# A gated cross-attention block: stacks loaded in 8 KB runs, attention inputs in two alternating buffers

## Chip, core and metric

The kernel runs on one core of a Trainium2 chip. The metric is device time in microseconds (us), from the first to the last instruction of one execution; a run's number is the median over repeated executions. Five compute engines run their own instruction streams: TensorE (PE, matrix products), VectorE (DVE), ScalarE (ACT), GpSimd (POOL), and SyncE (SP), which here issues every DMA. They wait for each other through semaphores. Sixteen DMA engines carry the transfers.

## What is computed

Thirty-two sequences of 128 tokens, width 256, go through one decoder layer (self-attention A, cross-attention B on `ctx`, feed-forward C) added with a tanh gate, and then a gated FFN (E) with ternary weights and quantised activations:

```python
def _mha(q_in, k_in, v_in, ..., mask):          # 16 heads of depth 16
    q, k, v = (split heads of q_in @ wq + bq, k_in @ wk + bk, v_in @ wv + bv)
    scores = einsum('bhqd,bhkd->bhqk', q, k) / sqrt(16)      # masked
    return (softmax(scores) @ v) merged @ wo + bo
def layer(x, enc):
    x = ln(x + mha(x, x, x, ...))               # A
    x = ln(x + mha(x, enc, enc, ...))           # B
    return ln(x + relu(x @ ff_w1 + b1) @ ff_w2 + b2)         # C
x = x + tanh(g_xattn) * layer(layernorm(x), ctx)
x = x + tanh(g_ffn) * bitlinear_ffn(layernorm(x))            # E
```

## The kernel before

Two sequences form a group (T = 256 tokens); there are 16 groups, and the program is a software pipeline written out in full. `ORDER` lists, for each engine, the steps of one iteration with a lag: the step (2, ("B", "Q")) works in iteration t on group t - 2. Every engine walks its own list in order, so one late step holds all that stands behind it. The end of an iteration on one engine need not be that of another. Sixteen groups and lags up to 4 give 20 iterations.

Every float32 product is made of three float16 products of a high and a low part (`products`, L560). For the attention scores both parts are put into one contraction: the stack `stk[s, "Q"]` has, for each of the 16 heads, in partitions 0 to 63 four blocks of 16 depth channels (high, high, low, low), and `stk[s, "K"]` has (high, low, high, low). Partitions 64 to 127 hold mask and row-maximum rows. A score product then contracts 128 partitions at once.

The projections come out with 128 channels of (head, depth) in the partitions, so they are brought into the stack's form through DRAM:

1. `prep` makes `qk_AQ`, `qk_AK`, `qk_BK`, `qk_BQ` (128 partitions; part, chunk, token). For A/Q and B/K the low part comes from POOL (L1309), for the others from DVE (L1106).
2. `parts_out` (L443) writes 256 KB to `part_dram` with rows of one channel, 256 tokens, 512 bytes.
3. `parts_in` (L453) waits for that write and loads 4 transfers for each stack, 16 partitions x 16 heads x 512 bytes = 128 KB each: 512 KB for a stack.
4. `scores_max` (PE, L631 and L635) multiplies them for the row maxima; DVE takes the maximum of each (L1126), PE transposes it (L645), ACT and DVE split it in two float16 rows (`mT`, L903 and L1131), and SP writes the two rows into partitions 126 and 127 of the Q stack (L464). Then `scores` (L657, L662) can run, and ACT takes the exponentials (L896, L898).

PE reaches the first B maximum (2, ("B","smax",0,0)) with the wait for both B stacks; its first A maximum (0, ("A","smax",0,0)) waits for both A stacks; (2, ("B","S",1,0)) waits for the second pair of `mT_B` rows.

The inputs of A, B and C are `hin` (h0, h1, h2), one buffer each. A residual is needed long after the input's buffer is wanted again, so SP copies h0 and h1 to `hres_A` and `hres_B` (step "hres", L482, 256 KB each) and `W` (DVE L1153) adds from there. On SP the two copies stand ahead of B's four transfer steps, and the copy for B waits until `W` of the group before has read the last copy (DVE L1153).

Before the pipeline starts, SP loads biases and weights, ACT makes the high and DVE the low parts of the eight attention matrices (L781, L981); DVE then makes the bias rows (L994 to L997).

Of the kernel before, what the change touches and what calls it, by code (L numbers as in the profile page):

```python
# [6 lines left out]
F32 = mybir.dt.float32  # L7
# [202 lines left out]
def build(nc, x, ctx_in, mask_x, mask_s, g_x, g_f, w, out):  # L210
    with ExitStack() as stack:
# [10 lines left out]
        part_dram = {(s, t): nc.dram_tensor(f"parts_{s}{t}", (2, D, T), F16).ap() for s in "AB" for t in "QK"}  # L222
# [43 lines left out]
        hin = {"A": sb("h0", [P, G, D], F32), "B": sb("h1", [P, G, D], F32), "C": sb("h2", [P, G, D], F32)}  # L266
        hT = {s: [sb(f"hT_{s}{q}", [P, DC, T], F16) for q in (0, 1)] for s in "ABC"}
        hres = {s: sb(f"hres_{s}", [P, G, D], F32) for s in "AB"}
# [84 lines left out]
        hres_in = {s: sem(f"hres_in_{s}") for s in "AB"}  # L353
# [57 lines left out]
        def _(eng):  # L411
# [4 lines left out]
            for name, width in BIASES:  # L416
                eng.dma_start(bf[:, BCOL[name]:BCOL[name] + width], w[name].partition_broadcast(1)).then_inc(u_dma, 16)
# [19 lines left out]
            def parts_out(s, name, g):  # L437

                split = (masked_lo[s], g.at(1, 1)) if (s, name) in MASKED else read((s, name), g)
                taken = g.at(64)  # L440
# [77 lines left out]
        def _(eng):  # L518
# [53 lines left out]
            def prep(step, g):  # L572
# [4 lines left out]
                if name in ("T", "X", "TQ"):  # L577
# [6 lines left out]
                    else:  # L584
                        src = hin[s]
# [33 lines left out]
            def scores_max(step, g):  # L619
# [320 lines left out]
        def _(eng):  # L940
# [176 lines left out]
            def unit_step(step, g):  # L1117
# [29 lines left out]
                elif what == "W":  # L1147
# [10 lines left out]
            def beside(step, g):  # L1158
                kind, k = step[1], step[2]
                if kind == "F2":  # L1160
# [4 lines left out]
                    eng.scalar_tensor_tensor(res["C"][:, k, :], bank[:, 0:D], 1.0 / (WS * WS), hin["C"][:, k, :],  # L1165
# [57 lines left out]
        def _(eng):  # L1223
# [41 lines left out]
            def run(step, g):  # L1265
# [10 lines left out]
                elif kind == "N":  # L1276
# [4 lines left out]
                    if s == "A":  # L1281
                        wait(eng, *full(("B", "T"), g.back(1)))
# [72 lines left out]
```

## Time and profile before

| | us |
|---|---|
| runs | 1186.05, 1198.15, 1199.59 |
| median | 1198.15 |
| profiled execution | 1203.71 |
| its span (first to last instruction) | 1201.2 |

| engine | busy us | share of the span |
|---|---|---|
| PE | 920.2 | 77% |
| DVE | 793.9 | 66% |
| ACT | 629.5 | 52% |
| POOL | 606.3 | 50% |

The mean granted clock of PE is 0.89 of full speed; the 16 DMA engines are 43% busy with the kernel's own transfers, 84.43 MB in 138160 packets. No engine is busy all the time, so the sum of busy times doesn't give the end: what counts is which wait ends last at each place of the pipeline. Matmul records are lost here and there (a few per cent), so a busy time of PE is rather too small.

### The profile page before, as it was taken

The numbers are of one execution on the slowest core, as the hardware profiler recorded it, in microseconds if no ns is written. First come the engines' busy times: TensorE is split into PE (matmuls) and PEld (weight loads), VectorE is DVE, ScalarE is ACT, GpSimd is POOL, SyncE is SP. The second block draws the span as 40 slices with busy tenths as digits, with TensorE's granted clock in tenths as the row PEclk, the third lists the DMA queues.
The fourth block names the chain that finished last, engine by engine and source line by source line (L and its number), as shares of the span: only waits on it lengthen the run. The fifth ranks groups of instructions, "written<-read, shape, count | busy, mean of one in ns | idle before, by whom it ended". The sixth has DMA issues, their size and how long they took to land.

```text
span 1201.2 us, 26870 instructions
## 1 busy us (share of the span) xinstructions
PE 920.2 (77%) x10076; PEld 736.4 (61%) x10147; DVE 793.9 (66%) x1887; ACT 629.5 (52%) x996; POOL 606.3 (50%) x740
## 2 busy tenths in 40 slices
PE   1155568788888888788788888788898878796774
PEld 1134456666776767667577667667676767574552
DVE  8644365477778686757668676767686766675654
ACT  2222344465566565646456555656575646473543
POOL 6013255474647473726456464747373736563520
PEclk9966779889899999988989879999999988997886
DMA  5444454536272635345444517354554545404000
GB/s 152 111 100 62 72 81 68 84 62 74 70 81 77 79 74 80 53 74 89 72 63 92 71 54 86 50 96 66 81 81 81 81 72 76 78 28 62 20 10 9
DMA packets 138286, 86.14 MB, mean 72 GB/s; under 512 B 12552, under 2 KB 133551, under 8 KB 138160
## 3 DMA queue, kind: packets, MB, share of 16 engines
q1 hardware_dynamic: 138160, 84.43, 43.3%
q8 instruction: 82, 1.34, 0.6%
q14 instruction: 44, 0.36, 0.1%
HBM read 54.49 MB, written 20.98 MB: 63 GB/s over the span
## 4 chain that ended last, share of the span: by engine, by line
PE 28%; DMA 21%; DVE 15%; issue 9%; POOL 6%; ACT 5%; SPq 5%; POOLq 0%; DVEq 0%; ACTq 0%
DMA stk_BQ<-parts_BQ 10%; DMA stk_BQ<-mT_B 5%; PE lin_B L560 4%; SPq L453 4%; PE st L662 3%; PE lin_C L560 3%; PE smax L635 3%; DMA parts_BK<-qk_BK 2%; PE lin_A L560 2%; POOL elo L1272 2%; DVE nm_B L1126 2%; PE st L657 2%; DVE amc L1077 2%; DMA parts_BQ<-qk_BQ 2%; ACT ehi L898 1%
## 5 line engine op out<-in xcount | busy, mean ns | idle before, releaser
L1272 POOL TENSOR_TENSOR elo<-e,ehi 128x1024 f16<-128x1024 f32 x128 | 272.2, 2130 | 187.3 <-ACT ehi L898 187.0
L896 ACT ACTIVATE e<-st 128x1024 f32<-128x1024 f32 x128 | 130.1, 1016 | 106.9 <-PE st L662 106.7
L1126 DVE TENSOR_REDUCE nm_B<-smax 128x4 f32<-128x512 f32 x128 | 87.9, 686 | 90.0 <-PE smax L635 89.8
L1126 DVE TENSOR_REDUCE nm_A<-smax 128x4 f32<-128x512 f32 x128 | 87.8, 686 | 88.1 <-PE smax L635 80.1
L898 ACT ACTIVATE ehi<-st 128x1024 f16<-128x1024 f32 x128 | 130.3, 1018 | 0.0
L1309 POOL TENSOR_TENSOR qk_AQ<-qf_A,qk_AQ 128x512 f16<-128x512 f32 x16 | 18.5, 1156 | 220.1 <-ACT qk_AQ L850 220.1
L1258 POOL TENSOR_TENSOR lrs<-lve,neghalf 128x1 f32<-128x1 f32 (+1 forms) x112 | 69.0, 616 | 114.9 <-DVE lve L1052 114.9
L635 PE MATMUL smax<-stk_BK,stk_BQ 126*128 126x128 f16 x512 | 55.2, 236 | 59.5 <-DMA stk_BQ<-parts_BQ 56.2
L631 PE MATMUL smax<-mb,ident_big 128*128 128x512 f16 x128 | 56.4, 440 | 51.1 <-issue 39.9
L883 ACT ACTIVATE late<-lin_E,hcg 128x512 f32<-128x512 f32 x32 | 21.7, 677 | 122.5 <-PE lin_E L721 121.6
L635 PEld LDWEIGHTS smax<-stk_BK,stk_BQ 126*128 126x128 f16 x512 | 38.0, 105 | 68.8 <-DMA stk_BQ<-parts_BQ 57.9
L568 PE MATMUL lin_B<-ones,brows 128*128 128x256 f16 x96 | 29.5, 308 | 45.8 <-DVE hT_B L1093 41.9
L662 PEld LDWEIGHTS st<-stk_AQ,stk_AK 128*128 128x128 f16 x512 | 45.7, 110 | 22.8 <-issue 10.6
L635 PEld LDWEIGHTS smax<-stk_AK,stk_AQ 126*128 126x128 f16 x512 | 45.7, 110 | 21.8 <-issue 9.1
L657 PE MATMUL st<-mbT,ident_big 128*128 128x512 f16 x128 | 56.8, 444 | 2.9 <-DMA stk_AQ<-mT_A 2.9
L635 PE MATMUL smax<-stk_AK,stk_AQ 126*128 126x128 f16 x512 | 57.9, 244 | 0.0
L662 PE MATMUL st<-stk_AQ,stk_AK 128*128 128x128 f16 x512 | 56.8, 241 | 0.0
L662 PE MATMUL st<-stk_BQ,stk_BK 128*128 128x128 f16 x512 | 43.8, 235 | 9.9 <-DMA stk_BQ<-mT_B 7.6
L874 ACT ACTIVATE late<-late,magic_col,s 128x1024 f32<-128x1024 f32 x32 | 39.5, 1236 | 21.6 <-DVE s L1192 21.6
L631 PEld LDWEIGHTS smax<-mb,ident_big 128*128 128x128 f16 x128 | 13.5, 105 | 61.0 <-issue 47.3
L676 PE MATMUL av<-vhi_A,ehi 128*128 128x17 f16 x512 | 45.2, 171 | 3.1 <-POOL elo L1272 1.5
L676 PE MATMUL av<-vhi_B,ehi 128*128 128x17 f16 x512 | 43.7, 171 | 2.8 <-POOL elo L1272 2.5
(293 smaller groups left out, 3016.5 us busy)
## 6 DMA issues: line engine op xcount, KB each, us to landing
stk_AQ<-parts_AQ SPq DMA_DIRECT2D x64, 128.0 KB, 4.7
stk_AK<-parts_AK SPq DMA_DIRECT2D x64, 128.0 KB, 7.1
stk_BK<-parts_BK SPq DMA_DIRECT2D x64, 128.0 KB, 4.8
stk_BQ<-parts_BQ SPq DMA_DIRECT2D x64, 128.0 KB, 7.0
x_a<-in_x_dram SPq DMA_DIRECT2D x16, 256.0 KB, 2.9
cx<-in_ctx_dram SPq DMA_DIRECT2D x16, 256.0 KB, 7.3
parts_AQ<-qk_AQ SPq DMA_DIRECT2D x16, 256.0 KB, 2.3
parts_AK<-qk_AK SPq DMA_DIRECT2D x16, 256.0 KB, 2.9
```

The costliest lines, as they stand in the source:

```text
L453: eng.dma_start(stk[s, name][DH * j:DH * (j + 1), :, :], part_dram[s, name][q].rearrange("(h d) n -> d h n", d=DH)).then_inc(stk_in[s, nam ...
L560: mm = eng.matmul(dst, lhs(a, k), rhs(b, k), start=(start and at == 0), stop=(at == last))
L631: eng.matmul(smax[:, :], ident_big[:, :], mb[:, :].unsqueeze(1).to_broadcast([P, 4, P]), start=True, stop=True)
L635: mm = eng.matmul(smax[:, i * P:(i + 1) * P], stk[s, "Q"][0:XROW, h, tok], stk[s, "K"][0:XROW, h, tok], start=(s == "B"), stop=True, skip_ ...
L657: eng.matmul(st[:, k2 * 512:(k2 + 1) * 512], ident_big[:, :], mbT[:, :].unsqueeze(1).to_broadcast([P, 4, P]), start=True, stop=True)
L662: mm = eng.matmul(st[:, col:col + P], stk[s, "K"][:, h, tok], stk[s, "Q"][:, h, tok], start=(s == "B"), stop=True, skip_group_check=True)
L676: eng.matmul(dst, ehi[:, hf, i * P:(i + 1) * P], vhi[s][:, b, h, :], start=True, stop=False, skip_group_check=True)
L896: eng.activation(e32[:, hf, :], st[:, :], ACT.Exp, scale=SCORE).then_inc(e32_ready, 1)
L898: eng.activation(ehi[:, hf, :], st[:, :], ACT.Exp, scale=SCORE).then_inc(drain, 1)
L1126: eng.tensor_reduce(nm[s][:, 4 * part:4 * part + 4], smax[:, :].rearrange("p (h k) -> p h k", h=4), AX_X, ALU.max, negate=True).then_inc(d ...
L1258: eng.tensor_tensor(lrs[n][:, a:b], lve[n][:, a:b], neghalf[:, 0:b - a], ALU.pow).then_inc(ln_pow[n], 1)
L1272: eng.tensor_tensor(elo[:, hf, :], e32[:, hf, :], ehi[:, hf, :], ALU.subtract).then_inc(elo_ready, 1)
```

## The change

It has three parts.

- **Channel order.** The columns of the query and key matrices (and their biases) are permuted while they are split into high and low parts, so that partition p of chunk c holds depth p // 8 and head 2 * (p % 8) + c. With `part_dram` laid out as (part, partition, chunk, token), the 16 heads of one depth channel lie in one run of 8 KB.
- **Transfers.** A Q stack loads in 2 transfers of 32 partitions x 8 KB, a K stack in one of 32 and two of 16 partitions. The write goes in 1 KB rows. The bias vectors of q and k are permuted by the DMA that loads them.
- **Inputs.** h0 and h1 have two buffers each, used by even and odd groups. `W` adds from the input itself; the copies, their waits and `hres_A`, `hres_B` are gone.

```diff
-        (0, ("A", "M", 0)), (4, ("E", "DN", 1, 2)), (1, ("B", "hres")), (0, ("A", "hres")), (1, ("B", "K")),
+        (0, ("A", "M", 0)), (4, ("E", "DN", 1, 2)), (1, ("B", "K")),
...
-        part_dram = {... (2, D, T), F16 ...}
+        part_dram = {... (2, P, DC, T), F16 ...}
...
+        def input_of(s, g):
+            return hin[s][g.const % len(hin[s])]
+        def by_depth(mat, m):
+            return mat[:, :, m * P:(m + 1) * P].rearrange("p c (d e) -> p c d e", d=DH)
+        def of_raw(mat, m):
+            return mat.rearrange("p (c e m d) -> p m c d e", c=DC, m=DC, d=DH)[:, m, :, :, :]
+        BY_DEPTH = (0, 1, 4, 5)
+        LOADS = {"Q": 32, "K": 48}
...
+                if name[-1] in "qk":
+                    eng.dma_start(dst.rearrange("p (m d e) -> p m d e", m=DC, d=DH),
+                                  w[name].rearrange("(o e m d) -> o m d e", o=1, m=DC, d=DH),
+                                  allow_slow_non_contiguous=True).then_inc(u_dma, 16)
...
-                eng.dma_start(part_dram[s, name].rearrange("q (c p) n -> p (q c) n", p=P),
-                              qk_parts[s, name][:, :, :]).then_inc(part_out[s, name], 16)
+                eng.dma_start(part_dram[s, name].rearrange("q p c n -> p q (c n)"),
+                              qk_parts[s, name][:, :, :].rearrange("p (q c) n -> p q (c n)", q=2)).then_inc(
+                                  part_out[s, name], 16)
...
-                for j in range(4):
-                    q = j // 2 if name == "Q" else j % 2
-                    eng.dma_start(stk[s, name][DH * j:DH * (j + 1), :, :],
-                                  part_dram[s, name][q].rearrange("(h d) n -> d h n", d=DH)).then_inc(stk_in[s, name], 16)
+                rows = part_dram[s, name].rearrange("q (d e) c n -> (q d) (e c n)", d=DH)
+                for first, src in ((0, 0), (32, 0)) if name == "Q" else ((0, 0), (32, 16), (48, 0)):
+                    n = 16 if (name, src) == ("K", 16) or first == 48 else 32
+                    eng.dma_start(stk[s, name][first:first + n, :, :].rearrange("r h n -> r (h n)"),
+                                  rows[src:src + n, :]).then_inc(stk_in[s, name], 16)
...
-                elif kind == "hres":
-                    source = (ln_out[0], g.at(1, 1)) if s == "A" else (ln_bias[1], g.at(G, G))
-                    taken = read((s, "W", G - 1), g.back(1))
-                    eng.wait_ge(*source)
-                    wait(eng, *taken)
-                    eng.dma_start(hres[s][:, :, :], hin[s][:, :, :]).then_inc(hres_in[s], 16)
...
                 # high_part (ACT), n in BY_DEPTH; else as before
+                    for m in range(DC):
+                        a_ = eng.activation(by_depth(dst, m), of_raw(raw[n], m), ACT.Copy, scale=WS)
...
                 # low_part (DVE), n in BY_DEPTH; else as before
+                    for m in range(DC):
+                        for c in range(DC):
+                            i_ = eng.scalar_tensor_tensor(by_depth(lo, m)[:, c, :, :], of_raw(raw[n], m)[:, c, :, :], WS,
+                                                          by_depth(hi, m)[:, c, :, :], ALU.mult, ALU.subtract)
...
-                    wait(eng, *full(("A", "T"), g.back(1)))
-                    wait(eng, hres_in["A"], g.at(16))
+                    wait(eng, *full(("A", "T"), g.back(2)))
+                    wait(eng, *read(("A", "W", G - 1), g.back(2)))
...
-                    eng.wait_ge(hres_in[s], g.at(16, 16))
-                    eng.scalar_tensor_tensor(res[s][:, b, :], bank[:, 0:D], 1.0 / WS, hres[s][:, b, :], ALU.mult,
+                    eng.scalar_tensor_tensor(res[s][:, b, :], bank[:, 0:D], 1.0 / WS, input_of(s, g)[:, b, :], ALU.mult,
```

On SP, the transfers around the stacks of B read before as follows (one iteration; a row is line, instruction, target <- source, shape, and how often in a row):

```order
L482 DMA hres_B<-h 128x512
L482 DMA hres_A<-h 128x512
L443 DMA parts_BK<-qk_BK 128x4x256
L476 DMA stk_BK<-maskrow 1x16x256
L443 DMA parts_BQ<-qk_BQ 128x4x256
L453 DMA stk_BK<-parts_BK 16x16x256 x4
L453 DMA stk_BQ<-parts_BQ 16x16x256 x4
L464 DMA stk_AQ<-mT_A 1x16x128 x2
```

With the change the same place reads:

```order
L459 DMA parts_BK<-qk_BK 128x2x512
L494 DMA stk_BK<-maskrow 1x16x256
L459 DMA parts_BQ<-qk_BQ 128x2x512
L471 DMA stk_BK<-parts_BK 32x4096
L471 DMA stk_BK<-parts_BK 16x4096 x2
L471 DMA stk_BQ<-parts_BQ 32x4096 x2
L482 DMA stk_AQ<-mT_A 1x16x128 x2
```

The two copies are gone, so the write of `parts_BK` is the first of the group, and the eight loads are five.

Ahead of the pipeline DVE makes the low parts of the matrices; `w_AQ`, `w_AK`, `w_BQ`, `w_BK` are the ones that are permuted. Before:

```order
L981 SCALAR_TENSOR_TENSOR w_AQ<-late,w_AQ 128x512
L981 SCALAR_TENSOR_TENSOR w_AK<-late,w_AK 128x512
L981 SCALAR_TENSOR_TENSOR w_AV<-late,w_AV 128x512
L990 TENSOR_TENSOR late<-late,lin_E 1x256
L981 SCALAR_TENSOR_TENSOR w_AO<-late,w_AO 128x512
L981 SCALAR_TENSOR_TENSOR w_BQ<-late,w_BQ 128x512
L981 SCALAR_TENSOR_TENSOR w_BK<-late,w_BK 128x512
```

And with the change:

```order
L1001 SCALAR_TENSOR_TENSOR w_AQ<-late,w_AQ 128x128 x4
L1001 SCALAR_TENSOR_TENSOR w_AK<-late,w_AK 128x128 x4
L1005 SCALAR_TENSOR_TENSOR w_AV<-late,w_AV 128x512
L1015 TENSOR_TENSOR late<-late,lin_E 1x256
L1005 SCALAR_TENSOR_TENSOR w_AO<-late,w_AO 128x512
L1001 SCALAR_TENSOR_TENSOR w_BQ<-late,w_BQ 128x128 x4
L1001 SCALAR_TENSOR_TENSOR w_BK<-late,w_BK 128x128 x4
```

Four whole-matrix instructions have become sixteen quarters, at the same places of the list.

## Rows read from the trace of the kernel before

**Rows 1.** Waits of PE, whole span: waiter, releaser, total us, times, longest.

```profile
PE smax L635 <- DMA stk_BQ<-parts_BQ: 56.2, 16, 5.8
PE lin_B L568 <- DVE hT_B L1093: 41.9, 16, 3.4
PE smax L631 <- issue: 39.9, 15, 6.1
```

**Rows 2.** SyncE timeline, first and last of 15 writes of parts_BQ from 200 us.

```profile
200.63 0.37 SPq L443 DMA_DIRECT2D parts_BQ<-qk_BQ  x1
...
1092.44 0.36 SPq L443 DMA_DIRECT2D parts_BQ<-qk_BQ  x1
```

**Rows 3.** Busy us by stretch (PE, PEld, DVE, ACT, POOL), PEclk, DMA share, GB/s.

```profile
387.88:449.31 61.43, 52.61 (x628) 43.56 (x631) 46.45 (x115) 38.08 (x62) 36.47 (x46) 0.97 0.49 79
...
582.05:651.03 68.98, 56.06 (x631) 45.56 (x634) 46.71 (x115) 38.23 (x62) 36.73 (x46) 0.90 0.45 70
```

**Rows 4.** Waits of PE in the stretch 387.88:449.31 (clock 0.97).

```profile
PE smax L635 <- DMA stk_BQ<-parts_BQ: 2.8, 1, 2.8
PE smax L631 <- issue: 1.8, 1, 1.8
```

**Rows 5.** SyncE timeline around B's stacks, one iteration: start us, us, what.

```profile
647.92 0.52 SPq L482 DMA_DIRECT2D hres_B<-h  x1
...
649.17 1.19 SPq L443 DMA_DIRECT2D parts_BK<-qk_BK  x1
...
651.03 0.54 SPq L443 DMA_DIRECT2D parts_BQ<-qk_BQ  x1
653.00 1.80 SPq L453 DMA_DIRECT2D stk_BK<-parts_BK  x4
654.90 1.86 SPq L453 DMA_DIRECT2D stk_BQ<-parts_BQ  x4
```

**Rows 6.** POOL timeline of the same iteration: the low part of B's keys.

```profile
645.74 1.15 POOL L1309 TENSOR_TENSOR qk_BK<-qf_B,qk_BK 128x512 f16<-128x512 f32 x1
```

**Rows 7.** PE timeline of the same iteration: the first maximum of B.

```profile
664.51 0.61 PE L635 MATMUL smax<-stk_BK,stk_BQ 126*128 126x128 f16 x4 [4.36 <-DMA stk_BQ<-parts_BQ]
```

**Rows 8.** DMA rate in 40 slices of 656:664, loads of B's stacks.

```profile
GB/s 84 97 103 141 120 97 97 92 95 146 126 100 92 90 100 138 128 92 97 87 95 146 126 102 97 90 87 143 128 100 92 97 80 78 108 0 0 0 0 0
```

**Rows 9.** The same for 652.0:653.2, writes of parts, 512-byte packets.

```profile
GB/s 17 34 17 102 154 222 273 307 273 324 290 324 290 290 290 324 307 290 307 256 290 273 273 273 273 273 324 239 358 307 307 256 205 205 205 137 68 290 17 34
```

**Rows 10.** The same for 12:25, weight loads, 1 and 4 KB packets, 128 partitions.

```profile
GB/s 183 129 73 60 26 4 0 0 0 0 19 230 378 388 381 378 394 375 366 347 350 347 350 347 350 353 353 353 356 394 391 416 403 416 403 391 366 88 0 0
```

**Rows 11.** SyncE timeline around A's stacks, the same iteration.

```profile
609.53 0.94 SPq L443 DMA_DIRECT2D parts_AK<-qk_AK  x1
611.64 1.80 SPq L453 DMA_DIRECT2D stk_AQ<-parts_AQ  x4
613.54 1.87 SPq L453 DMA_DIRECT2D stk_AK<-parts_AK  x4
...
617.46 1.15 SPq L464 DMA_DIRECT2D stk_BQ<-mT_B  x2
```

**Rows 12.** PE timeline: the first maximum of A.

```profile
623.13 0.59 PE L631 MATMUL smax<-mb,ident_big 128*128 128x512 f16 x1 [3.08 <-issue]
```

**Rows 13.** DMA issues of the page: KB each, median us from issue to landing.

```profile
parts_BQ<-qk_BQ SPq DMA_DIRECT2D x16, 256.0 KB, 2.9
...
stk_BQ<-mT_B SPq DMA_DIRECT2D x64, 4.0 KB, 2.1
```

**Rows 14.** Stretch 6:7, `bvcol` loads: busy share in tenths by slice, packets.

```profile
DMA  0000011011221222122122222222221121121121
...
DMA packets 358, 0.00 MB, mean 1 GB/s; under 512 B 358, under 2 KB 358, under 8 KB 358
```

**Rows 15.** Timeline of the set-up: first ACT instruction, a low part on DVE.

```profile
17.09 1.28 ACT L781 ACT_TABLE_LOAD   x1 [17.09 <-DMA late<-in_L_xattn_s_wq_dram]
...
25.56 0.69 DVE L981 SCALAR_TENSOR_TENSOR w_AQ<-late,w_AQ 128x512 f16<-128x512 f32 x1
```

More of the change, by code:

```diff
@@ L221, in build @@
         out_v = out.rearrange("(g b) p d -> g b p d", b=G)
-        part_dram = {(s, t): nc.dram_tensor(f"parts_{s}{t}", (2, D, T), F16).ap() for s in "AB" for t in "QK"}
+        part_dram = {(s, t): nc.dram_tensor(f"parts_{s}{t}", (2, P, DC, T), F16).ap() for s in "AB" for t in "QK"}
         maskrow_dram = nc.dram_tensor("maskrow", (NG, T), F16).ap()
@@ L265, in build @@
         cx = sb("cx", [P, G, D], F32)
-        hin = {"A": sb("h0", [P, G, D], F32), "B": sb("h1", [P, G, D], F32), "C": sb("h2", [P, G, D], F32)}
+        hin = {"A": [sb(f"h0_{q}", [P, G, D], F32) for q in (0, 1)], "B": [sb(f"h1_{q}", [P, G, D], F32) for q in (0, 1)],
+               "C": [sb("h2", [P, G, D], F32)]}
         hT = {s: [sb(f"hT_{s}{q}", [P, DC, T], F16) for q in (0, 1)] for s in "ABC"}
-        hres = {s: sb(f"hres_{s}", [P, G, D], F32) for s in "AB"}
         qk_parts = {(s, t): sb(f"qk_{s}{t}", [P, 2 * DC, T], F16) for s in "AB" for t in "QK"}
@@ L439, in parts_out @@
                 split = (masked_lo[s], g.at(1, 1)) if (s, name) in MASKED else read((s, name), g)
-                taken = g.at(64)
+                taken = g.at(LOADS[name])
                 wait(eng, stk_in[s, name], taken)
                 eng.wait_ge(*split)
-                eng.dma_start(part_dram[s, name].rearrange("q (c p) n -> p (q c) n", p=P),
-                              qk_parts[s, name][:, :, :]).then_inc(part_out[s, name], 16)
+                eng.dma_start(part_dram[s, name].rearrange("q p c n -> p q (c n)"),
+                              qk_parts[s, name][:, :, :].rearrange("p (q c) n -> p q (c n)", q=2)).then_inc(
+                                  part_out[s, name], 16)
             def parts_in(s, name, g):
@@ L584, in prep @@
                     else:
-                        src = hin[s]
+                        src = input_of(s, g)
                         if s == "A":
@@ L780, in high_part @@
                 eng.wait_ge(u_raw[n], 16)
-                eng.activation(dst[:, :, :].rearrange("p c n -> p (c n)"), raw[n], ACT.Copy, scale=WS).then_inc(u_hi, 1)
+                if n in BY_DEPTH:
+                    for m in range(DC):
+                        a_ = eng.activation(by_depth(dst, m), of_raw(raw[n], m), ACT.Copy, scale=WS)
+                    a_.then_inc(u_hi, 1)
+                else:
+                    eng.activation(dst[:, :, :].rearrange("p c n -> p (c n)"), raw[n], ACT.Copy, scale=WS).then_inc(u_hi, 1)
             eng.wait_ge(u_const, N_CONST)
@@ L817, in prep @@
                     eng.wait_ge(ln_rstd[0], g.at(1, 1))
-                    wait(eng, *full(("A", "T"), g.back(1)))
-                    wait(eng, hres_in["A"], g.at(16))
-                    normalize(0, range(G), lambda k: x_a[:, k, :], lambda k: hin["A"][:, k, :])
+                    wait(eng, *full(("A", "T"), g.back(2)))
+                    wait(eng, *read(("A", "W", G - 1), g.back(2)))
+                    normalize(0, range(G), lambda k: x_a[:, k, :], lambda k: input_of("A", g)[:, k, :])
                     return
@@ L1281, in run @@
                     if s == "A":
-                        wait(eng, *full(("B", "T"), g.back(1)))
-                        wait(eng, hres_in["B"], g.at(16))
+                        wait(eng, *full(("B", "T"), g.back(2)))
+                        wait(eng, *read(("B", "W", b), g.back(2)))
                     else:
                         wait(eng, *read(("C", "F2", b), g.back(1)))
-                    eng.tensor_tensor(hin[nxt][:, b, :], tg[s][:, b, :], lnb[n][:, :], ALU.add).then_inc(ln_bias[n], 1)
+                    eng.tensor_tensor(input_of(nxt, g)[:, b, :], tg[s][:, b, :], lnb[n][:, :], ALU.add).then_inc(ln_bias[n], 1)
                 elif kind == "stat":
```

17 lines of the change are left out of this document (11 added, 6 removed).

## Prediction

> **What bounds the kernel now.** I read the shares of busy time first: PE 77%, DVE 66%, nobody full. So the length of an iteration is set by waits, and the view to go to is the waits of PE, the busiest engine. Over the whole span three of them are large [rows 1]: 56.2 us for the loads of B's query stack (16 times), 41.9 us for DVE's `hT_B`, and 39.9 us "issue" at L631. That last one isn't issue time: L631 is the first instruction of A's row maximum, behind the wait for both A stacks, and its DMAs run until it starts [rows 11, 12]. So some 96 us of PE's idle time are waits for stacks.
>
> Next the period. `parts_BQ` is written once per iteration; 15 of these writes, 14 periods, lie between 200.63 and 1092.44 [rows 2], 63.7 us each on average. They aren't equal: 61.43 us in a stretch whose granted clock is 0.97, 68.98 us in one with 0.90 [rows 3]. In the quick one PE still waits 2.8 us for the B stack and 1.8 us for the A stacks [rows 4]; in the slow one 4.36 and 3.08 us [rows 7, 12], and the clock falls to its lower level of 1.2 GHz for several us behind such pauses. I expect a period without the stack waits to look like the quick one less its two waits.
>
> **Why the stacks are late.** While B's stacks load, the DMA engines move about 110 GB/s [rows 8]. The writes of the parts, with the same 512-byte packets but 128 partitions, move about 290 [rows 9], and weight loads with 1 and 4 KB packets into 128 partitions 350 to 410 [rows 10]. So packets of 512 B alone don't explain 110. What is different in the stack loads is that a transfer ends in 16 partitions. I take it that the rate goes with the partitions reached: about 110 GB/s for 16, 220 for 32. The Trainium skill, "SBUF — State Buffer", section "Door 1: The DMA port swizzle", gives a cause: partitions 0 to 15 reach 4 of 16 ports (109 GB/s), 0 to 31 reach 8 (218 GB/s). The trace agrees for 16 partitions; for 32 no row here shows it. By that page the longer runs alone bring nothing, and K's two loads of 16 partitions stay slow; my sum has the same shape. The bounds by rows are 110 (nothing gained) and 410.
>
> **B's stacks, step by step** (the slow iteration). Before: `hres_B` goes out at 647.92, held until DVE's W has read the last copy; then `hres_A`, and `parts_BK` only at 649.17, though POOL has `qk_BK` ready at 645.74 + 1.15 = 646.9 [rows 5, 6]. K loads start to be issued at 653.00, the last Q load lands and PE goes on at 664.51, having stood since 660.15 [rows 7]. With the change:
> - `parts_BK` goes out at about 646.9, 2.3 us earlier, and is landed when `parts_BQ` is ready at 651.03, which doesn't move.
> - K's three issues (0.45 us each, 1.80 for four) follow at 651.5. Their data come behind the write of `parts_BQ`, from about 652.9: 256 KB at 220 and 2 x 128 KB at 110 GB/s, 1.2 us each, until 656.5.
> - `parts_BQ` is landed at 651.03 + 2.9 = 653.9 [rows 13]; Q's two issues end at 654.8. Its data, 2 x 256 KB at 220 GB/s, run to 658.9. Before, data ended at 663.0 (35 of 40 slices of rows 8) and PE went on 1.5 us later, so Q is usable at about 660.2.
> - PE wants it at 660.15. The wait of 4.36 us shrinks to between 0 and 0.5. At 410 GB/s there would be slack, and the time would be the same. At 110 GB/s 1 MB takes 9.5 us from 652.9 and 2 to 3 us of wait stay.
>
> **A's stacks.** `parts_AK` goes out at 609.53 [rows 11], unmoved (DVE sets it). Q's two loads follow, data from 611.5 to 613.9; K's issues wait for the landing of `parts_AK` at 612.4 and need 1.4 us, their data run from 613.6 to 617.2, usable at 618.7. PE wants them at 623.13 - 3.08 = 620.05: nothing left to wait, 1.3 us of slack. `cx` lies behind K in the queues, to 617.9. `mT_B`, issued 617.46 to 618.6, comes back in its normal 2.1 us [rows 13], 620.7 at the latest, when PE asks (620.5).
>
> **What doesn't bring time by itself.** The copies' 8 MB are 32 transfers of 0.7 us each beside other work; their worth is only the earlier `parts_BK`, and that is in B's sum. The second input buffers remove waits that were long over (two groups back instead of one); POOL and ACT don't show a wait there. `W` adds from another buffer of the same shape and costs the same. New waits: the input's writer waits for `W` of the group two back, which is an iteration old and more; it holds nothing. PE's list doesn't move.
>
> **What is left.** The quick period gives 61.43 - 2.8 - 1.8 = 56.8 us. DVE is busy 46.5 us of it, PE 52.6 [rows 3], and the 3.4 us wait for `hT_B` stays [rows 1]: 52.6 + 3.4 = 56.0, so 56.8 can be had, but nearly nothing under it. I add 0.5 for a rest of stack waits and short clock drops behind the `hT_B` pause: 57.3. Over 14 periods (63.7 - 57.3) x 14 = 90 us. Two more loads of B's stack lie outside them, at the start and at the end, 4.5 us each: 9.
>
> **Set-up.** Twelve more DVE instructions. A quarter matrix costs between 0.17 (a quarter of 0.69 us) and 0.69 us [rows 15]; nearer a quarter with its start, 0.3. Four matrices then cost 4 x (1.2 - 0.69) = 2 us, all on the path, as DVE's low parts run back to back into the bias rows. ACT's halves cost about as much, but ACT runs ahead of DVE there. The permuted bias loads are 4 x 256 elements of 4 bytes. The nearest row is `bvcol`, also 4-byte pieces: 358 packets in 1 us on 16 engines at a busy share near 0.15 [rows 14], so 7 ns of engine time and at most 45 ns of wall time each. Spread over all engines, 1024 pieces cost 0.5 to 3 us, hidden ahead of the weights, which ACT waits for until 17.09. If only one engine carried them, the weights behind them would come up to 46 us later. I take 2 us seen, so +4 in all; the range gets up to +20. The skill, "DMA: Bandwidth & Descriptors", section "Why a DMA increments its semaphore by 16 and not by 1", says that the engines used divide both patterns' slowest dimension, which here would be two engines, and its rules say a strided last dimension gives one descriptor per element. This speaks against the change: by it and the row's 7 to 45 ns, 512 pieces on an engine would take 4 to 23 us, and the set-up would come out at +5 to +20.
>
> **Sum**, against the profiled execution's own 1203.7 us: 1203.7 - 90 - 9 + 4 = 1109. The median of the runs is 0.46% below that execution, so about 1104.
>
> **Rivals.**
> - *The rate stays.* 8 KB rows into 16 or 32 partitions move no faster than 110 GB/s. For it: nothing in the trace shows a transfer into 32 partitions. Against it: 110 to 290 to 410 follow partitions. Then only the earlier `parts_BK` counts, some 1.5 us x 15 = 23, less 4: 1203.7 - 19 = 1185, as a median 1179, within 2%. Chance 0.12.
> - *The wait is taken over.* With PE early, DVE (46.5 us of 57) and POOL's `elo` decide who is late, or the pause at `hT_B` now meets a lower clock in most iterations (0.90 instead of 0.97 is 0.07 x 69 = 5 us of PE's speed in a period [rows 3]). Then the period is 60 to 61: 1203.7 - 38 to 52 - 9 + 4, a median of about 1150. For it: the 68.98 us periods themselves come of such drops. Against: the 61.43 us period has the 3.4 us pause and keeps 0.97. Chance 0.17.
> - *Slower.* A row of 8 KB written by one DMA engine into one partition is slower than sixteen rows of 512 B. It decides against the change where the stack loads land more than (24 + 99) / 15 = 8 us later than in my sum, which is below about 65 GB/s for the 1 MB of a pair. At 60 GB/s, 17.5 us for B's pair, PE would stand some 7 us at B and 5 at A instead of 4.4 and 3.1: about 1235. Nothing in the trace shows such a rate for large packets; chance 0.04.
>
> **Chances.** 0.67 for my forecast, whose own range is 1080 to 1130 (period 56 to 58.5, set-up +2 to +20), 0.17 for about 1150, 0.12 for about 1179, 0.04 slower. 2% of 1198 is 24 us, about what a measurement tells from no change, so faster means under 1174: 0.67 + 0.17 + a third of 0.12 = 0.88; within 2%: 0.08; slower 0.04. The range for 8 in 10 reaches from 1080 over the second case to 1160.
>
> **What would show it.** In the profile after: stack transfers at about 220 GB/s for 32 and 110 for 16 partitions; `parts_BK` issued when POOL's L1309 part ends; PE's wait for `stk_BQ` under 10 us in total instead of 56.2, "issue" at L631 under 10 instead of 39.9; the `hT_B` wait unchanged near 42; periods of 56 to 59 us; a mean clock above 0.93; first PE instruction of the pipeline (43 us before) within 2 to 20 us later. I am wrong if the stack rate is 110 all along, if the set-up grows by tens of us, or if the waits for stacks vanish and the period stays above 60.

## The result, and the profile after

| | before | with the change |
|---|---|---|
| median of the runs, us | 1195.13 (4 runs, 1186.05 to 1199.59) | 1072.97 (4 runs, 1067.78 to 1076.88) |
| profiled execution, us | 1203.71 | 1076.88 |
| its span, us | 1201.2 | 1075.0 |
| mean granted clock of PE | 0.89 | 0.92 |

The ratio is 0.898, with a 95% interval of 0.893 to 0.903. The change saves 122 us; I had forecast some 94, a time of 1104, and 1072.97 lies 7 us below the low end of my range, 1080.

First the page of the kernel after: busy time by engine, and the loads of B's query stack (count, KB each, median us from issue to landing).

```profile
PE 883.3 (82%) x10076; PEld 715.0 (67%) x10147; DVE 791.7 (74%) x1899; ACT 630.2 (59%) x1000; POOL 606.0 (56%) x740
...
stk_BQ<-parts_BQ SPq DMA_DIRECT2D x32, 256.0 KB, 5.8
```

DVE, ACT and POOL are busy as long as before (793.9, 629.5 and 606.3 us then). Only PE's own busy time fell, from 920.2 to 883.3 us, with the same list of products: its matmuls ran faster, which is the clock.

Next the waits of PE over the whole span (waiter, releaser, total us, times, longest), to be read beside [rows 1].

```profile
PE lin_B L580 <- DVE hT_B L1118: 40.6, 16, 3.4
...
PE st L669 <- DMA stk_AQ<-mT_A: 4.4, 7, 1.0
...
PE st L674 <- DMA stk_BQ<-mT_B: 4.2, 7, 1.4
...
PE smax L643 <- issue: 4.2, 2, 3.3
...
PE smax L647 <- DMA stk_BQ<-parts_BQ: 2.5, 1, 2.5
```

The wait for B's query stack went from 56.2 us in 16 waits to 2.5 us in one, the "issue" in front of A's maxima (L631 before, L643 now) from 39.9 to 4.2. The wait for `hT_B` stayed (41.9, now 40.6) and is the largest that is left.

The writes of `parts_BQ` mark the periods, as in [rows 2]. SyncE's timeline after (start us, us, what), first and last of the 15 from 190 us on:

```profile
194.11 0.37 SPq L459 DMA_DIRECT2D parts_BQ<-qk_BQ  x1
...
969.34 0.36 SPq L459 DMA_DIRECT2D parts_BQ<-qk_BQ  x1
```

Fourteen periods take 775.2 us, 55.4 each, where they took 891.8, 63.7 each. Of the 126.2 us by which the span is shorter, 116.6 are there, 6.5 ahead of the first write and 3.1 behind the last. The same stretch by windows (us, then busy us of PE, PEld, DVE, ACT and POOL with counts, PEclk, DMA share, GB/s), before:

```profile
200.63:1092.44 891.81, 748.15 (x8605) 612.87 (x8667) 625.55 (x1557) 520.08 (x835) 506.15 (x625) 0.93 0.47 74
```

and after, with one single period under it:

```profile
194.11:969.34 775.23, 711.98 (x8605) 591.97 (x8667) 621.38 (x1557) 518.77 (x835) 505.88 (x625) 0.97 0.33 75
...
585.40:639.69 54.29, 50.87 (x628) 42.54 (x631) 45.05 (x115) 38.05 (x62) 36.45 (x46) 1.00 0.35 80
```

PE's busy time for the same 8605 matmul records fell by 36.2 us, the clock rose from 0.93 to 0.97. In this stretch the two stack waits had been 46.9 us (B, 14 times) and 30.2 us (A, 13 times), and after neither is listed there. 77.1 and 36.2 make 113.3 of the 116.6 us. So, read from these two executions, about a third of the gain isn't the waits that went away but the higher clock of the work around them.

### The profile page after: what moved, and what is told of

Its sections match the earlier page's. It is cut to its first block, busy times and chain, and to the rows that moved or that the text cites. A ratio compares the mean times of both kernels' runs of the same rounds, so it can differ in the third digit from the quotient of the medians.

```text
span 1075.0 us, 26722 instructions
## 1 busy us (share of the span) xinstructions
PE 883.3 (82%) x10076; PEld 715.0 (67%) x10147; DVE 791.7 (74%) x1899; ACT 630.2 (59%) x1000; POOL 606.0 (56%) x740
## 4 chain that ended last, share of the span: by engine, by line
PE 44%; DVE 15%; issue 9%; POOL 7%; ACT 6%; DMA 6%; SPq 1%; POOLq 0%; DVEq 0%; ACTq 0%
PE lin_B L572 6%; PE lin_A L572 5%; PE lin_E L572 4%; PE st L674 4%; PE lin_C L572 4%; PE smax L647 3%; DMA stk_AQ<-mT_A 3%; POOL elo L1296 2%; PE st L669 2%; DVE amc L1102 2%; DMA stk_BQ<-mT_B 2%; ACT ehi L915 2%; DVE nm_B L1151 2%; ACT e L913 1%; PE lin_B L580 1%
## 5 line engine op out<-in xcount | busy, mean ns | idle before, releaser
L1333 POOL TENSOR_TENSOR qk_AQ<-qf_A,qk_AQ 128x512 f16<-128x512 f32 x16 | 18.5, 1155 | 156.2 <-ACT qk_AQ L867 156.2
L580 PE MATMUL lin_B<-ones,brows 128*128 128x256 f16 x96 | 29.2, 304 | 44.6 <-DVE hT_B L1118 40.6
L643 PE MATMUL smax<-mb,ident_big 128*128 128x512 f16 x128 | 53.5, 418 | 14.9 <-DVE nm_A L1151 10.2
L647 PEld LDWEIGHTS smax<-stk_AK,stk_AQ 126*128 126x128 f16 x512 | 43.1, 104 | 19.9 <-issue 5.6
L647 PE MATMUL smax<-stk_BK,stk_BQ 126*128 126x128 f16 x512 | 50.7, 222 | 6.6 <-DMA stk_BQ<-parts_BQ 2.5
L669 PE MATMUL st<-mbT,ident_big 128*128 128x512 f16 x128 | 50.9, 397 | 4.5 <-DMA stk_AQ<-mT_A 4.4
L647 PE MATMUL smax<-stk_AK,stk_AQ 126*128 126x128 f16 x512 | 54.1, 232 | 0.0
L674 PEld LDWEIGHTS st<-stk_AQ,stk_AK 128*128 128x128 f16 x512 | 41.0, 101 | 18.4 <-issue 2.5
L674 PE MATMUL st<-stk_AQ,stk_AK 128*128 128x128 f16 x512 | 51.2, 224 | 0.0
L580 PEld LDWEIGHTS lin_B<-ones,brows 128*128 128x128 f16 x96 | 10.1, 105 | 56.8 <-issue 43.0
L674 PE MATMUL st<-stk_BQ,stk_BK 128*128 128x128 f16 x512 | 40.1, 222 | 6.5 <-DMA stk_BQ<-mT_B 4.2
L692 PE MATMUL av<-vhi_A,elo 128*128 128x17 f16 x512 | 45.0, 171 | 0.0
```

The lines of the kernel that those rows point to most:

```text
L580: eng.matmul(dst, brows[:, col:col + P], ones16[:, 0:tokens], start=True, stop=False)
L643: eng.matmul(smax[:, :], ident_big[:, :], mb[:, :].unsqueeze(1).to_broadcast([P, 4, P]), start=True, stop=True)
L647: mm = eng.matmul(smax[:, i * P:(i + 1) * P], stk[s, "Q"][0:XROW, h, tok], stk[s, "K"][0:XROW, h, tok], start=(s == "B"), stop=True, skip_ ...
L669: eng.matmul(st[:, k2 * 512:(k2 + 1) * 512], ident_big[:, :], mbT[:, :].unsqueeze(1).to_broadcast([P, 4, P]), start=True, stop=True)
L674: mm = eng.matmul(st[:, col:col + P], stk[s, "K"][:, h, tok], stk[s, "Q"][:, h, tok], start=(s == "B"), stop=True, skip_group_check=True)
```

## The experiments

Each ratio is against the kernel before on the same chip, with its 95% interval. The theory that they test: the stack loads are paced by the partitions that a transfer reaches, PE's waits for them set the period, the copies bring little. The rivals: the copies or the shorter rows are what counts, or another wait takes over.

**e1: the kernel before without its copies.** Inputs in two buffers, `W` adds from the input, the stack transfers as before.

```diff
 # ORDER["SP"]
-(0, ("A", "M", 0)), (4, ("E", "DN", 1, 2)), (1, ("B", "hres")), (0, ("A", "hres")), (1, ("B", "K")),
+(0, ("A", "M", 0)), (4, ("E", "DN", 1, 2)), (1, ("B", "K")),
...
 # W, DVE
-eng.wait_ge(hres_in[s], g.at(16, 16))
...
-eng.scalar_tensor_tensor(res[s][:, b, :], bank[:, 0:D], 1.0 / WS, hres[s][:, b, :], ALU.mult,
+eng.scalar_tensor_tensor(res[s][:, b, :], bank[:, 0:D], 1.0 / WS, input_of(s, g)[:, b, :], ALU.mult,
```

> The kernel before with only the third part of the change: two input buffers, no copies; stacks still load as 4 transfers of 16 partitions x 16 x 512 B. Theory (the gain is the stacks' landing time, set by the partitions a transfer reaches): only the write of parts_BK moves ahead, PE's wait for stk_BQ falls from 56 us to about 30, the A wait stays near 40; 1160 to 1175 us. Rival (the 8 MB of copies in the DMA queues were what held things up): below 1130 us and stack landings clearly under 7 us.

Measured: 1187.6 us, ratio 0.989 (0.984 to 0.995), 13.5 us saved, which is under 2% but clear of no change. Waits of PE, whole span:

```profile
PE smax L631 <- DMA stk_BQ<-parts_BQ: 45.6, 16, 5.9
PE smax L627 <- issue: 41.5, 15, 6.0
```

The B wait lost 10.6 us of 56.2, the A wait nothing. An earlier `parts_BK` helps little while the 1 MB of the pair takes almost 9 us of data: the end of the loads hangs on the rate and on `parts_BQ`, which hasn't moved. I had expected two to three times as much. Taken alone, dropping the copies is worth about a ninth of the change's gain.

**e2: the change with the copies kept.** The reverse of e1, in the kernel after: one buffer for each input, copies and their waits back in their old places.

```diff
-(0, ("A", "M", 0)), (4, ("E", "DN", 1, 2)), (1, ("B", "K")),
+(0, ("A", "M", 0)), (4, ("E", "DN", 1, 2)), (1, ("B", "hres")), (0, ("A", "hres")), (1, ("B", "K")),
...
```

> The changed kernel with the copies put back: one input buffer each, both copies ahead of parts_BK on SyncE; loads in 8 KB runs. Theory: the stacks come 1.5 to 2 us later at B, which uses up the slack there, some 0.5 us of wait returns in an iteration; 1075 to 1095 us. Rival (the inputs carry the gain): above 1130 us.

Measured: 1077.2 us, ratio 0.899 (0.895 to 0.903), beside 0.898 (0.893 to 0.903) for the full change. The wait for B's query stack is 6.1 us in 5 waits instead of 2.5 in one. With the transfers in their new form there is slack in front of B, and what the copies take falls mostly into it. e1 and e2 together: the layout and the transfers carry the gain, the copies between nothing and some 13 us, depending on whether the loads are late anyway.

**e3: rows of 8 KB, but 16 partitions for each transfer.** Four transfers for a stack as before.

```diff
-LOADS = {"Q": 32, "K": 48}
+LOADS = {"Q": 64, "K": 64}
...
-for first, src in ((0, 0), (32, 0)) if name == "Q" else ((0, 0), (32, 16), (48, 0)):
-    n = 16 if (name, src) == ("K", 16) or first == 48 else 32
+for first, src in ((0, 0), (16, 0), (32, 16), (48, 16)) if name == "Q" else ((0, 0), (16, 16), (32, 0), (48, 16)):
+    n = 16
```

> The changed kernel with each stack in 4 transfers of 16 partitions x 8 KB. Theory (partitions reached set the rate): the rate stays near 110 to 140 GB/s, half the stack waits of before return, and lower clock behind them; 1110 to 1150 us. Rival (the length of the runs sets the rate): 1070 to 1080 us, as with 32 partitions.

Measured: 1120.84 us, ratio 0.936 (0.932 to 0.940). Waits of PE, and the DMA rate in 40 slices of 0.4 us from the issue of `parts_BQ`'s write (543.55:559.55):

```profile
PE smax L647 <- DMA stk_BQ<-parts_BQ: 19.9, 15, 4.0
PE smax L643 <- issue: 18.6, 15, 5.1
...
GB/s 21 0 256 338 389 287 41 287 41 143 184 0 287 41 123 205 0 246 82 123 205 0 12 49 0 0 0 0 0 0 0 0 0 0 0 0 0 0 0 0
```

The time is where the theory had it, but both waits are under half of what they were before, and the rate will turn out above the 110 to 140 GB/s expected: the longer rows help at 16 partitions as well. e4 turns the question round.

**e4: the partitions of the change, but rows of 512 bytes.** Even and odd heads are loaded apart, so every run in DRAM is one head's 256 tokens; ten transfers for a pair.

```diff
-LOADS = {"Q": 32, "K": 48}
+LOADS = {"Q": 64, "K": 96}
...
-    eng.dma_start(stk[s, name][first:first + n, :, :].rearrange("r h n -> r (h n)"),
-                  rows[src:src + n, :]).then_inc(stk_in[s, name], 16)
+    for c in range(DC):
+        eng.dma_start(stk[s, name][first:first + n, :, :].rearrange("r (e c) n -> r c e n", c=DC)[:, c, :, :],
+                      rows[src:src + n, :].rearrange("r (e c n) -> r c e n", c=DC, n=T)[:, c, :, :]).then_inc(
+                          stk_in[s, name], 16)
```

> The changed kernel with the same partitions in each transfer, but even and odd heads apart, so that every run is 512 B (twice as many transfers: 4 for Q, 6 for K). Theory: 32-partition transfers move about 200 GB/s also with 512 B runs, five more issues of 0.45 us cost about 1 us of landing; 1075 to 1100 us. Rival (run length): the rate falls back to 110 GB/s and the time to 1130 us or more.

Measured: 1098.71 us, ratio 0.915 (0.912 to 0.919). The two stack waits, the rate (535.77:551.77) and SyncE's issues of the same place:

```profile
PE smax L649 <- DMA stk_BQ<-parts_BQ: 15.2, 12, 4.1
...
PE smax L645 <- issue: 8.5, 7, 3.9
...
GB/s 0 0 266 340 78 224 172 214 137 96 87 170 69 113 101 228 128 245 196 159 220 42 13 41 0 1 0 0 0 0 0 0 0 0 0 0 0 0 0 0
...
536.23 3.82 SPq L472 DMA_DIRECT2D stk_BK<-parts_BK  x6
540.15 2.49 SPq L472 DMA_DIRECT2D stk_BQ<-parts_BQ  x4
```

For comparison the same 16 us of e1, whose transfers are those of before (510.31:526.31):

```profile
GB/s 0 0 201 284 213 257 172 138 142 101 92 137 100 96 134 102 95 138 99 92 141 99 92 152 91 84 53 9 4 0 0 0 0 41 0 0 0 0 0 0
```

and of the kernel after (529.65:545.65), with SyncE and PE in this iteration:

```profile
525.32 0.37 SPq L459 DMA_DIRECT2D parts_BK<-qk_BK  x1
...
530.11 1.34 SPq L471 DMA_DIRECT2D stk_BK<-parts_BK  x3
531.84 0.77 SPq L471 DMA_DIRECT2D stk_BQ<-parts_BQ  x2
...
539.50 0.38 PE L647 MATMUL smax<-stk_BK,stk_BQ 126*128 126x128 f16 x4
...
GB/s 0 0 266 325 392 164 410 143 184 143 123 205 61 205 164 225 225 48 14 0 0 0 41 0 0 0 0 0 0 0 0 0 0 0 0 0 0 0 0 0
```

In each row the first 262 KB are the write, and what follows is the pair's 1 MB (1.05 million bytes). Counted from where the write's bytes are used up to the last large slice, it takes about 8.7 us with 16 partitions and 512-byte rows (e1, 121 GB/s), 6.8 us with 16 partitions and 8 KB rows (e3, 154), 6.7 us with the partitions of the change and 512-byte rows (e4, 156), and 5.2 us with both (after, 200). Over thirteen iterations of each run the order is the same: 7.8 to 8.9, 6.2 to 7.0, 6.5 to 7.8 and 5.1 to 5.7 us.

A slice can hold parts of several transfers. What one transfer takes is read better from the landings of the query stack's loads: in the kernel after, the two are issued at 531.8 and 532.2 us and land 5.1 and 5.9 us later.

```profile
L471 SPq DMA_DIRECT2D stk_BQ<-parts_BQ x2: 302/362/422, 531.8 to 532.2; - x2
...
DMA to landing us min/median/max: 5.1/5.5/5.9
```

The same two lines for the query stack's four loads of e1, of e3 and of e4, each from the same iteration as above:

```profile
L455 SPq DMA_DIRECT2D stk_BQ<-parts_BQ x4: 392/444/447, 513.1 to 514.6; - x4
...
DMA to landing us min/median/max: 6.1/7.2/7.9
```

```profile
L471 SPq DMA_DIRECT2D stk_BQ<-parts_BQ x4: 368/420/421, 545.9 to 547.3; - x4
...
DMA to landing us min/median/max: 5.5/6.3/6.9
```

```profile
L472 SPq DMA_DIRECT2D stk_BQ<-parts_BQ x4: 542/607/608, 540.2 to 542.0; - x4
...
DMA to landing us min/median/max: 3.1/3.3/3.4
```

From one landing to the next it is 1.2 us for 256 KB in the kernel after, but 1.1 us for only 128 KB in e1 and 0.9 us for 128 KB in e3 (medians over all iterations: 1.1, 1.1 and 0.9). So a transfer into 32 partitions brings 1.7 to 2 times as much in the same time as one into 16, much as the theory says. But e3 shows that the rows count too: into the same 16 partitions 8 KB rows go in some 0.9 us where 512-byte rows take 1.1, and the pair moved a quarter faster (154 against 121). Whether that comes from fewer packets or from neighbouring transfers, into different partitions, overlapping more, these runs don't tell.

e4 can't give the rate of 512-byte rows into 32 partitions, only a lower bound. Its loads land a steady 3.1 to 3.4 us after their issue, the last as soon as the first, while in e1 they queue up and land 6.1 to 7.9 us after it. So in e4 SyncE sets the pace: ten issues take 6.3 us (five take 2.1 in the kernel after; I had counted 0.45 us for one), and one in 0.62 us is some 210 GB/s for Q's 128 KB transfers and 102 for K's 64 KB ones, which is what its slices hold there (196 in the 16th to the 21st, 106 in the 10th to the 15th). e4's 26 us over the kernel after are therefore at least in part the issues, not the row length.

With e1, e3, e4 and the kernel after, none of which has the copies, the two effects can be set side by side, as shares of the time before:

| saved | 16 partitions | 32 (K: 32 and 16) |
|---|---|---|
| 512-byte rows | 1.1% (e1) | 8.5% (e4, held back by its issues) |
| 8 KB rows | 6.4% (e3) | 10.2% (after) |

Either one alone gets most of the way, and they don't add up. e1 also keeps the write in 512-byte rows: that of `parts_BQ` lands after 2.8 us by the median there and after 2.2 in the kernel after, and the pair's data start some 0.3 us later behind it. That is small beside the 3.5 us by which the two differ in the data themselves. Not tried was a load into 32 partitions with the old channel order.

**e5: the kernel before with ten dummy products (128x512) on PE ahead of its wait for B's stacks.** Their output, in `smax`, is overwritten. This asks what a pause costs besides its own length.

```diff
+if s == "B" and (b, quad) == (0, 0):
+    wait(eng, drain, before)
+    for i in range(10):
+        eng.matmul(smax[:, :], ident_big[:, :], mb[:, :].unsqueeze(1).to_broadcast([P, 4, P]), start=True, stop=True)
 if quad == 0:
     for t in "QK":
```

> The kernel before, with ten extra products of 512 columns (2.2 us at full clock) on PE just ahead of the wait for B's stacks, written over afterwards: the wait stays as long as it was, but PE is busy for most of it. Theory (a stall costs its own length and then the lower clock behind it): the measured wait for stk_BQ shrinks by about 2 us each, nothing of this is time won, but drops of the clock behind it become rarer, mean clock 0.92 or more, and the kernel is 10 to 35 us faster than before although it does more. Rival (the lower clock costs nothing on the path, the gain of the change is only the stalls themselves): same time or up to 10 us slower.

Measured: 1186.71 us, ratio 0.989 (0.983 to 0.994). The wait for B's stack over the whole span and the steady stretch by windows:

```profile
PE smax L640 <- DMA stk_BQ<-parts_BQ: 17.4, 14, 3.1
...
199.58:1077.31 877.73, 770.71 (x8809) 617.44 (x8807) 622.35 (x1557) 519.60 (x835) 506.30 (x625) 0.95 0.48 75
```

PE does more work, gets nothing earlier, and the kernel is 13 us shorter (under 2%, but the interval leaves out no change): the clock of the stretch is 0.95 instead of 0.93, the period 62.7 instead of 63.7 us. The mean clock of the whole execution is 0.91, just short of the 0.92 that I had expected. Part of what a stack wait costs is therefore the slower work behind it.

**e6: the kernel after, three small DVE operations made one column at a time.** `amc`, `hcg` and `kap` (128x2) stand directly ahead of `hT_B` on DVE. In the period shown they take about three to seven times what they took where they were quickest (0.17, 0.21 and 0.22 us). The timelines of DVE and POOL in the kernel after, and `amc`'s durations in it (ns: shortest, median, longest):

```profile
633.12 1.24 DVE L1102 TENSOR_SCALAR amc<-am 128x2 f32<-128x2 f32 x1
...
634.47 0.56 DVE L1106 TENSOR_SCALAR hcg<-amc,kg 128x2 f32<-128x2 f32 x1
635.07 0.75 DVE L1108 SCALAR_TENSOR_TENSOR kap<-hcg,ku,amc 128x2 f32<-128x2 f32 x1
635.75 0.68 DVE L1118 TENSOR_TENSOR hT_B<-lin_E,hT_B 128x512 f16<-128x512 f32 x1
...
632.21 2.12 POOL L1296 TENSOR_TENSOR elo<-e,ehi 128x1024 f16<-128x1024 f32 x1
634.30 0.71 POOL L1303 TENSOR_TENSOR tg_B<-nrm_B,lng 128x256 f32<-128x256 f32 x1
635.09 0.72 POOL L1311 TENSOR_TENSOR h<-tg_B,lnb 128x256 f32<-128x256 f32 x1
...
L1102 DVE TENSOR_SCALAR amc<-am x16: 169/1255/1925, 238.9 to 1048.7; 128x2 f32<-128x2 f32 x16
```

`amc` ends (634.36) when POOL's `elo` ends (634.33), `hcg` (635.03) with the next POOL instruction (635.01), `kap` (635.82) with the one after (635.81). It isn't chance: over the kernel these are 48 instructions, and 44 of them end within 0.04 us of the end of a POOL instruction; the other four have none beside them and are the quickest.

The edit (`hcg` is split like `amc`, and `kap` is also written with two scalars for each partition instead of a second input):

```diff
-eng.tensor_scalar(amc[:, :], am1[:, :], 1e-5, 1.0 / QMAX, ALU.max, ALU.mult).then_inc(q_small, 1)
+for k in range(G):
+    i_ = eng.tensor_scalar(amc[:, k:k + 1], am1[:, k:k + 1], 1e-5, 1.0 / QMAX, ALU.max, ALU.mult)
+i_.then_inc(q_small, 1)
...
-eng.scalar_tensor_tensor(kap[:, :], hcg[:, :], ku[:, 0:1], amc[:, :], ALU.mult, ALU.mult).then_inc(q_small, 1)
+for k in range(G):
+    i_ = eng.tensor_scalar(kap[:, k:k + 1], hcg[:, k:k + 1], ku[:, 0:1], amc[:, k:k + 1], ALU.mult, ALU.mult)
+i_.then_inc(q_small, 1)
```

> The changed kernel, with the three small 128x2 VectorE instructions ahead of hT_B (amc, hcg, kap) each split in two of 128x1, the last with a per-partition scalar in place of its second tensor. Theory (what is left of PE's waits, 3.4 us for hT_B in an iteration, is on the path, and it is so long because these instructions end only when a GpSimd instruction beside them ends): amc, hcg, kap fall from up to 1.9, 0.7, 1.1 us to 0.2 to 0.4 us, the wait for hT_B from 41 to below 20 us in all; 1030 to 1055 us. Rival (another wait takes its place, or the GpSimd instructions have nothing to do with it): 1065 to 1080 us.

Measured: 1038.24 us (1037.04 to 1042.45), ratio 0.865 (0.861 to 0.868), the fastest kernel here. Durations of two of the operations in e6, the wait of PE, the steady stretch:

```profile
L1103 DVE TENSOR_SCALAR amc<-am x32: 142/149/155, 237.7 to 1008.5; 128x1 f32<-128x1 f32 x32
...
L1113 DVE TENSOR_SCALAR kap<-hcg,ku,amc x32: 264/268/274, 238.3 to 1009.3; 128x1 f32<-128x1 f32 x32
...
PE lin_B L580 <- DVE hT_B L1123: 11.8, 16, 1.7
...
191.00:932.04 741.04, 704.89 (x8669) 582.55 (x8667) 592.87 (x1599) 519.36 (x835) 505.17 (x625) 1.00 0.35 79
```

Twice as many instructions, each steady, and together 15.7 us instead of 45.0 over the kernel; the wait for `hT_B` falls by 28.8 us, and the time by about 35 (by the two ratios, each against its own runs of the kernel before, by 40). The rest fits PE's busy time in the steady stretch, 704.9 instead of 712.0 us at a clock of 1.00 instead of 0.97, and somewhat more than that for each record, as e6's stretch holds 64 more of them. The Trainium skill, "SBUF — State Buffer", section "Who interferes with whom", says that VectorE and GpSimd share one pair of ports, that a `tensor_scalar` in a two-port mode and a GpSimd instruction hold it against each other for a whole instruction, and that an operation with two SBUF inputs contends with a GpSimd instruction that reads SBUF. The rows agree: the 128x2 forms end with POOL's instruction, the 128x1 forms vary by no more than 13 ns, though a POOL instruction runs beside 45 of their 48 pairs.

**e7: the kernel after with twelve dummy products ahead of PE's wait for `hT_B`** in (B, Q), the counterpart of e5.

```diff
 src = hT[s]
+if step == ("B", "Q"):
+    for i in range(12):
+        eng.matmul(bank[:, :], ident_big[:, :], mb[:, :].unsqueeze(1).to_broadcast([P, 4, P]), start=True, stop=True)
 eng.wait_ge(*read((s, src_name), g))
```

> The changed kernel with twelve extra products of 512 columns (2.6 us) on PE ahead of the wait for hT_B, written over afterwards. Theory of the clock: in the changed kernel the drops that are left start behind this pause, so they get rarer, mean clock in the steady part above 0.98, and the time falls by 5 to 20 us. Rival (the pause doesn't set the clock, or the clock isn't on the path): same time within 5 us or slower.

Measured: 1067.85 us (1064.66 to 1068.93), ratio 0.888 (0.884 to 0.892).

```profile
PE lin_B L580 <- DVE hT_B L1122: 6.5, 10, 0.7
...
195.81:961.30 765.49, 738.68 (x8835) 597.53 (x8835) 623.70 (x1557) 520.66 (x835) 506.59 (x625) 1.00 0.34 76
```

The dummy products fill the wait, they don't shorten it, yet the clock is 1.00 and the period 54.7 instead of 55.4 us. So some 0.7 us of the kernel after's period is lower clock behind the `hT_B` pause. By the medians it is 5 us of the whole, against 35 in e6, by the ratios 12 against 40: most of what e6 took is the pause itself.

## Why the prediction was right, and where it wasn't

**Stack rate (right for 32 against 16 partitions, wrong on the rows).** In 512-byte rows 16 partitions move about 110 to 121 GB/s (e1), and 32 at least 196 (e4). In the kernel after, Q's transfers of 256 KB land 1.2 us apart, about 218, where I had 220. The pair's data took 5.2 us where I had 6.0 (652.9 to 658.9). The Trainium skill, "SBUF — State Buffer", section "Door 1: The DMA port swizzle", gives 109 and 218; these rows agree. Where I followed it to "the longer runs alone bring nothing", e3 says otherwise: 6.8 instead of 8.7 us, the two waits at 38.5 us instead of 96.1, and 80 us saved without a single 32-partition transfer (up to 13 of them are the copies). With 8 KB rows the wider transfers add some 45 us to that.

**B's and A's stacks (right).** `parts_BK` goes out at 525.32, when POOL's low part is ready (its L1333 ran until 525.25); the issues take 1.34 and 0.77 us; the last Q load, issued by 532.6, lands 5.8 us later by the median in the profile's DMA issues, at about 538.2; PE starts the first maximum at 539.50, 9.9 us behind the write of `parts_BQ`, without a wait. I had both at 9.1 us behind that write; it was 8.6 and 9.9. At A 4.2 us of "issue" are left over the whole kernel. So a transfer time 0.8 us too long hardly showed at B, where PE came later than the data in either case.

**Copies (right).** e2: within the measurement. "Their worth is only the earlier `parts_BK`" holds. For e1 I had still expected 1160 to 1175. The prediction's own 1.5 us a period (23 us) gives 1175, and even that is too much: measured was 0.7 us less wait per iteration and 13.5 us in all.

**Periods (the step that failed).** The term for a period without stack waits was too large, because it kept PE's busy time of a stretch in which part of the work ran at the lower clock. I wrote 61.43 - 2.8 - 1.8 = 56.8 "but nearly nothing under it", since 52.6 + 3.4 = 56.0, and added 0.5. Measured: 55.4 on average, 54.29 in the one shown above. The term was 1.9 us too large, 27 us over 14 periods:
- The 52.6 us that PE is busy weren't a floor. Windows of 1 us of the kernel before, right behind the 2.8 us wait of that quick stretch (PE goes on at 400.07):

```profile
400.00:401.00 1.00, 0.71 (x5) 0.59 (x7) 0.40 (x1) 0.00 (x0) 0.00 (x0) 0.62 0.00 0
401.00:402.00 1.00, 1.00 (x6) 0.52 (x5) 0.84 (x2) 0.00 (x0) 0.00 (x0) 0.50 0.00 0
402.00:403.00 1.00, 1.00 (x9) 0.72 (x7) 0.14 (x1) 0.00 (x0) 0.00 (x0) 0.50 0.00 0
403.00:404.00 1.00, 1.00 (x11) 0.90 (x9) 0.42 (x1) 0.00 (x0) 0.00 (x0) 0.67 0.00 0
404.00:405.00 1.00, 1.00 (x11) 0.89 (x10) 0.97 (x4) 0.00 (x0) 0.00 (x0) 1.00 0.00 0
```

  PE is busy there at 1.2 GHz for a little over 3 us, and about 1.7 us of speed are gone (52.61 against 50.87 us for 628 records at 1.00). I took the wait out of the stretch and left the slow work behind it in. In the kernel after, the other pause, at `hT_B`, still costs clock: read by the microsecond, the stretch has ten drops, all at or close behind that pause, 43 us at the lower clock together (one short drop in e6, and one in e7). So on average 0.65 us of the 1.7 come back: 711.98 / 8605 is 82.7 ns for a record, 52.61 / 628 is 83.8.
- I counted the `hT_B` wait with 3.4 us, its longest, which is also what it was in the quick stretch; the mean in the stretch after is 39.2 / 14 = 2.8. That is 0.6.
- The 0.5 for leftovers and drops came on top of a stretch that already held a drop: counted twice.

These make 1.75 of the 1.9 us. The three are read from profiles; no run changes one of them by itself.

**Outside the periods.** I had -9 for two more stack loads and +4 for the set-up, -5. Measured -6.5 ahead of the first write and -3.1 behind the last, -9.6. The loads were worth more than 9: outside the periods PE's wait for B's stack fell from 9.3 to 2.5 us, and A's, which the sum left out, from 9.7 to 4.2. The set-up term was +2, not +4: ACT's first instruction and DVE's quarters in the timeline after,

```profile
18.52 1.28 ACT L795 ACT_TABLE_LOAD   x1 [18.52 <-DMA late<-in_L_xattn_s_wq_dram]
...
25.57 1.20 DVE L1001 SCALAR_TENSOR_TENSOR w_AQ<-late,w_AQ 128x128 f16<-128x128 f32 x4
```

against [rows 15]. Four quarters take 1.20 instead of 0.69 us, as assumed, 2 us over four matrices. The weights come 1.4 us later, which is about the added issue time of the four permuted bias loads on SyncE (0.60 to 0.70 us each instead of 0.22 to 0.32, 1.5 us together). It is hidden: DVE starts at 25.57 instead of 25.56. PE's first product of the pipeline stands at 45.20 instead of 43.15. The rule of the Trainium skill, "DMA: Bandwidth & Descriptors", section "Why a DMA increments its semaphore by 16 and not by 1", by which +5 to +20 would have followed, isn't borne out as a price here.

**The rivals and signs.** The rate didn't stay, and no wait took over: `hT_B` kept its 41 us. Of the signs that I had named, the periods (55.4, not 56 to 59 us) and the mean clock (0.92 in the profiled execution, not above 0.93) didn't come. My range ended too high because its shortest period, 56 us, rested on the same "nearly nothing under it"; 55.4 us in the periods and 5 us less outside them lie below it.

**What isn't shown.** The split of 77 us of waits and 36 us of clock is read from two profiled executions; e5 and e7 show the clock's part at two pauses apart (13 us, and 5 to 12 us of time), not its whole. Why 8 KB rows into 16 partitions are quicker stays open.

## What to carry to other kernels

When a stack or tile loads slowly, look at how many partitions one transfer reaches and at the length of its rows; here either one brought more than half of the gain. A permutation of weight columns that is paid once in the set-up can buy long rows. Before you split a load, compare the bytes of one transfer with the time of its issue: 64 KB in 0.64 us is all that e4's smallest loads could move. When you remove a pause of PE, count the slow matmuls behind it as well, and never take the busy time of a stretch with a granted clock under 1 as a floor. When a tiny VectorE operation varies by a factor of ten, see whether it ends with a GpSimd instruction, and try the same work in another form, such as one column at a time.

## What the runs showed of the hardware that I had not expected

- Dummy products ahead of a wait shorten the kernel: 13 us in e5, 5 to 12 us in e7, with a granted clock of 0.95 instead of 0.93 and 1.00 instead of 0.97.
- A 128x2 operation on DVE took up to 1.93 us and 0.17 at its shortest; as two 128x1 operations it takes 0.14 to 0.16 us each, all 32 times. Three such operations were worth 35 us of 1073.
- With 16 partitions for each transfer, a pair of stacks in rows of 8 KB moved at about 154 GB/s and in rows of 512 bytes at about 121. With 32 partitions, 256 KB landed every 1.1 to 1.2 us in rows of 8 KB, and 512-byte rows reached at least 196 GB/s, held back by SyncE's 0.62 us for an issue.
